# Audio tower on one core: the rolled steady-state loop written out as straight-line iterations

## The reference

```
out = einsum('blfd,fd,fdk->blk', windows(x, 8 taps), filt, W);  h = relu(out + b_k)      # 248 rows x 64
h = h + attention(layernorm(h))      # one head of width 64; softmax over 248 keys; Wo
g = layernorm(h);  logits = g @ Wg + bg + bias;  top 2 of 8 experts, softmax of the two
h = h + sum over experts of combine[e] * (relu(g @ W1[e] + b1[e]) @ W2[e] + b2[e])       # hidden 128
```

## Time and profile before

| | |
|---|---|
| median of 3 runs | 343.15 us (342.94 to 343.67) |
| span of the profiled execution, first to last instruction | 340.8 us |
| PE busy | 307.6 us, 90% of the span, 1486 matmul records |
| DVE busy | 248.6 us, 73% |
| ACT busy | 240.9 us, 71% |
| POOL busy | 92.8 us, 27% |
| granted TensorE clock, mean | 0.959 of full speed |

### The profile page before, as it was taken

How to read it: one execution, slowest core, us unless ns; L and a number is a source line. 1 busy time by engine, 2 the same in 40 slices (tenths; PEclk the granted TensorE clock), 3 DMA queues, 4 the chain that set the end, 5 groups by cost and what they waited for, 6 DMA issues and landing times.

```text
span 340.8 us, 6412 instructions
## 1 busy us (share of the span) xinstructions
PE 307.6 (90%) x1486; PEld 188.0 (55%) x1486; DVE 248.6 (73%) x824; ACT 240.9 (71%) x545; POOL 92.8 (27%) x85
## 2 busy tenths in 40 slices
PE   8587799999999999999999999999999999979754
PEld 8264657565645657475656556474656565534220
DVE  2574747879696979779786969697887979492823
ACT  2427497969686887879686978778786969764520
POOL 1103031513232241515122322315151323132302
PEclk9767899999999999999999999999999999999985
DMA  6120214070614225160706142241707060504050
GB/s 181 50 61 0 63 58 124 17 182 5 159 37 124 73 78 119 29 168 5 191 1 151 45 130 67 81 116 26 171 9 187 2 164 0 147 21 126 12 136 15
DMA packets 17228, 28.38 MB, mean 83 GB/s; under 512 B 3264, under 2 KB 13760, under 8 KB 17216
## 3 DMA queue, kind: packets, MB, share of 16 engines
q1 hardware_dynamic: 16928, 27.98, 32.6%
q10 hardware_dynamic: 288, 0.28, 0.2%
HBM read 21.90 MB, written 2.29 MB: 71 GB/s over the span
## 4 chain that ended last, share of the span: by engine, by line
PE 40%; DVE 22%; issue 16%; ACT 11%; DMA 7%; SPq 1%; DVEq 1%; ACTq 0%; POOL 0%
PE bank_a L787 11%; DMA cb<-weights 5%; DVE ts L252 4%; PE bank_y L846 4%; PE bank_s L897 4%; PE bank_h L836 3%; PE bank_h L837 3%; ACT p L367 3%; ACT hid L376 2%; PE bank_b L904 2%; PE bank_s L804 2%; DVE hsum L637 2%; DVE acc L548 2%; DVE gw L617 2%; PE bank_h L867 2%
## 5 line engine op out<-in xcount | busy, mean ns | idle before, releaser
L376 ACT ACTIVATE hid<-bank_h,col 128x496 f32<-128x496 f32 x128 | 84.0, 674 | 10.5 <-PE bank_h L837 9.2
L846 PE MATMUL bank_y<-hid,w_sb 128*64 128x496 f32 x256 | 68.0, 612 | 3.6 <-DVE acc L548 3.6
L836 PE MATMUL bank_h<-xs,w_hi 128*128 128x496 f32 x128 | 56.2, 439 | 3.0 <-DVE xs L253 2.4
L548 DVE SCALAR_TENSOR_TENSOR acc<-bank_y,col,cb 128x496 f32<-128x496 f32 x64 | 45.4, 730 | 17.3 <-DMA cb<-weights 9.8
L837 PE MATMUL bank_h<-xs,w_lo 128*128 128x496 f32 x128 | 49.8, 389 | 0.0
L262 POOL TENSOR_TENSOR total<-acc 128x496 f32<-128x496 f32 x16 | 20.1, 1256 | 106.7 <-DVE acc L548 106.7
L330 POOL TENSOR_TENSOR p<-p,rmask 124x496 f32<-124x496 f32 x32 | 32.4, 1014 | 51.9 <-DVE rmask L564 51.8
L265 POOL TENSOR_TENSOR total<-total,acc 128x496 f32<-128x496 f32 x16 | 20.0, 1250 | 70.5 <-DVE acc L548 70.5
L836 PEld LDWEIGHTS bank_h<-xs,w_hi 128*128 128x128 f32 x128 | 24.3, 190 | 13.4 <-issue 7.1
L718 DVE SCALAR_TENSOR_TENSOR h<-bank_s,col,h 128x248 f32<-128x248 f32 x16 | 7.6, 476 | 31.9 <-PE bank_s L897 31.9
L367 ACT ACTIVATE p<-bank_s,nmax 124x248 f32<-124x248 f32 x64 | 29.4, 466 | 0.3 <-DVE nmax L555 0.2
(11 more groups left out here) (105 smaller groups left out, 584.8 us busy)
## 6 DMA issues: line engine op xcount, KB each, us to landing
cb<-weights SPq DMA_DIRECT2D x64, 248.0 KB, 4.5
kk<-kk SPq DMA_DIRECT2D x16, 248.0 KB, 2.9
x<-xt SPq DMA_DIRECT2D x15, 256.0 KB, 2.9
out<-h SPq DMA_DIRECT2D x16, 124.0 KB, 1.8
w_sb<-w SPq DMA_DIRECT2D x3, 256.0 KB, 3.6
wtok_sb<-wtok SPq DMA_DIRECT2D x1, 256.0 KB, 2.7
x<-xt ACTq DMA_DIRECT2D x1, 256.0 KB, 3.9
weights<-ct_sb SPq DMA_DIRECT2D x16, 15.5 KB, 1.4
```

The costliest lines, as they stand in the source:

```text
L376: act.activation(hid[2 * (p % 2) + s][:, :], bank_h[s][:, 0:TOK], ACT.Relu, bias=col[:, C_B1 + e:C_B1 + e + 1]).then_inc(hid_ready[s], 1)
L548: dve.scalar_tensor_tensor(out=acc[p % 2][:, :], in0=bank_y[p % 2][:, 0:TOK], scalar=col[:, C_B2 + p:C_B2 + p + 1], in1=cb[:, p, :], op0=A ...
L836: pe.matmul(bank_h[e % 2][:, 0:TOK], w1_hi[:, e, :], xs[par][:, :], start=True, stop=False)
L846: last = pe.matmul(bank_y[p % 2][s * D:s * D + D, 0:TOK], w2_sb[:, 2 * p + s, :], hid[2 * (p % 2) + s][:, :], start=True, stop=True)
```

## The change

The hardware loop goes. `run` calls `iteration` twenty times with Python integers. The flags of each iteration, the order of the work on every engine, the tiles and the awaited values are the same as before. No register is computed, no branch is taken, every wait compares with a constant, and the DRAM addresses of `x` and `out` are constants.

```
-        def run(iteration, eng):
-            iteration(-2, 0, True, False, False, False, False)
-            iteration(-1, 1, True, True, False, False, False)
-            iteration(0, 0, True, True, True, False, False)
-            iteration(1, 1, True, True, True, True, False)
-            with eng.Fori(0, (GROUPS - 4) // 2) as i:
-                iteration(i * 2 + 2, 0, True, True, True, True, True)
-                iteration(i * 2 + 3, 1, True, True, True, True, True)
-            iteration(GROUPS - 2, 0, False, True, True, True, True)
-            iteration(GROUPS - 1, 1, False, False, True, True, True)
-            iteration(GROUPS, 0, False, False, False, True, True)
-            iteration(GROUPS + 1, 1, False, False, False, False, True)
+        def run(iteration):
+            for t in range(-2, GROUPS + 2):
+                iteration(t, t % 2, t + 2 < GROUPS, -1 <= t < GROUPS - 1, 0 <= t < GROUPS, 1 <= t <= GROUPS, t >= 2)
...
-            run(iteration, sp)
+            run(iteration)
```

More of the change, by code:

```diff
@@ L347, in iteration @@
                     add(pool, m, 1)
-            run(iteration, pool)
+            run(iteration)
         @block.scalar
@@ L478, in iteration @@
                     exps(c, 0)
-            run(iteration, act)
+            run(iteration)
         @block.vector
@@ L761, in iteration @@
                     both_weights(n)
-            run(iteration, dve)
+            run(iteration)
         @block.tensor
@@ L989, in iteration @@
                     hidden(n, odd, 0)
-            run(iteration, pe)
+            run(iteration)
 def constants():
```

## The result

The changed kernel takes 334.93 us (median of 4 runs, 334.6 to 335.2). The kernel before, run beside it, took 343.41 us. The ratio is 0.9734, with a 95% interval of 0.9702 to 0.9766. All ratios here are those on record, which compare the fast executions of both kernels, and can differ by some 0.2% from the quotient of two medians.

What follows compares the result with a forecast made beforehand. A ring of waits through DVE, PE and ACT, closing once an iteration, was taken as the bound. From 343.15 us, 3.65 (branches), 1.2 and 0.6 (registers) came off and 1.7 (fetches) was added: 339.4 us, range 336.7 to 342.4.

Steps and rivals of the forecast that it cites:

- Taken branches: Loop turns, where DVE's branch lies bare on the ring of engines: five crossings at 0.73 us, 3.65 us less.
- The even beat: Sign: PE's weight load L904 recurs every 18.2 us or so, no longer at 18.35 and 19.08 us.
- Register instructions: Ahead of waits in twelve iterations: 0.10 us each at PE's L836, 0.05 at ACT's L376; 1.2 and 0.6 us less.
- DVE's other register instructions stand under a running instruction: Step that costed DVE's remaining register instructions at nothing, as running work covers them.
- More code to fetch: Straight code brings some 9 more queue-8 packets that delay awaited DMA transfers: net 1.7 us more, bounds -1.7 to 5.4.
- the 0.50 us left over: Part of the 206.00 us from iteration 2 to 13 beyond the regular intervals, read as a stretched gate-weight store's price.
- the price of a hit: Cost of a code packet falling on a transfer the ring waits for: 0.5 to 1.7 us, taken as 0.6.
- the chance of a hit: Share of an iteration in which a code packet meets an awaited transfer: 6.4 of 18.2 us, 0.35.
- the late hit in iteration 14: Packet at 294 us beside `cb`, DVE idle 1.74 us; might move away, chance about a third, 0.5 us subtracted.
- the fetches are hidden: Rival: all code fetches fall into slack, 337.7 us; chance 0.18.
- Only the branches matter: Rival: semaphore instructions replace the register ones at the same price, 341.2 us; chance 0.22.
- slower: Rival: each queue-8 packet holds the gate weights' round trip through DRAM, 348.5 us at 1.2 us each; chance 0.10.

Runs made afterwards that it cites:

- The moved code: The changed kernel with 40 already met waits added on PE in its first iteration, so later code packets shift: 335.10 us against 344.55 for the kernel before, ratio 0.9724.

## Why the prediction was right, and where it failed

The forecast missed by 339.4 - 334.9 = 4.5 us, and I had given only 0.02 to a time under 336.7. By its own terms:

*Taken branches, 3.65 us: right.* The even beat is there, L538 starts 0.13 us after L619, and the wait for `cb` is gone. DVE straightened alone removes the pause, PE or ACT alone do not, as the argument had it. With the loop gone the intervals across a turn are as short as the others, which is the 5 x 0.73 us; 0.2 of each 0.73 goes with SP straight alone.

*Register instructions, 12 x 0.15 = 1.8 us: the size was 2.93, and the place was wrong.* I put 0.10 on PE's L836 and 0.05 on ACT's L376, and DVE's and SP's at nothing. Both local readings came true: DVE's low part of `xs` is now followed by PE after 0.11 us (before 0.24), and PE's first layer by ACT after 0.04 (before 0.12). But PE straight alone has the quick start at L836 and keeps the 18.37 us beat, and with DVE and SP alone in straight code, PE and ACT as before, the beat is already 18.12 us. So of the 0.27 us, 0.23 are DVE's and SP's (DVE's 0.21 by the quietest interval of DVE alone, 18.14), and 0.04 come with the other three engines. The step that failed is "DVE's other register instructions stand under a running instruction". The kernel's own rows spoke against it: from PE's weight load to the end of DVE's gating there are 13.19 us before (181.76 to 194.95) and 12.97 after (178.09 to 191.06), in which DVE doesn't wait for `cb`. (The idle time of 0.59 and 0.86 us that I read as PE's is that of its weight loads; its matmuls stood 0.19 and 0.45 us there.) I looked for registers at the one link in which a gap stood open, and not at the sum over DVE's stretch. Of the 0.22 us of that stretch 0.09 lie ahead of the first weighing (3.88 us behind the weight load before, 3.79 after); the rest wasn't split further.

*More code to fetch, +1.7 us: the failed step that weighs most.* It came out as -2.0 us, if all that changed there is put down to it: nothing in the loop's time, the 0.50 us left over gone, and 1.49 us less behind it. This is 3.7 of the 4.5 us. The number of packets was right, and the price of a hit was, if anything, too low (DVE waited 1.2 to 2.1 us at each hit in the kernels with PE, or all but SP, straight). What failed is the chance of a hit. I took it from the kernel before, with a `cb` issued 0.97 us ahead of the beat in odd iterations and 1.4 in even ones, and multiplied: nine packets, 0.35 of the time exposed. For that I had counted all of the 5.0 us from `cb`'s issue to its use, while a packet that began 3.1 us or more behind the issue made the first half late in no trace. And the same change that brings the packets lets SP issue `cb` at 1.35 us in every iteration, and in that place packets did nothing (in the forecast's own words, the rival's "new ring with 0.2 us more slack on SP"). With SP's loop kept, four of them hit and ate all of the gain in the loop. The stores that I had counted as exposed did no harm either: three in the loop's time took 1.9 to 2.1 us with no effect, and a fourth, 2.5 us in iteration 15, put `cb` 0.2 us later. The moved code shows that SP's straight code is no shield by itself: one packet in the wrong place still cost 0.7 us. That the four fell just behind that place is luck that I hadn't forecast.

*The 1.49 us behind the loop.* I had given the late hit in iteration 14 a chance of a third to move away. It moved: the queues there list no packet of queue 8, and DVE's idle time before the first weighing is 0.79 us, not 1.74. Eight of the ten kernels that keep PE's loop have that packet, with a second `cb` transfer of 5.2 us or more; those with PE straight have 4.1 to 4.5. So this part (0.95 us) is PE's, and it is a matter of where the packets happen to fall. The other 0.5 us weren't traced; the granted clock behind iteration 13 is 0.92 before and 0.93 after.

*The 0.50 us left over, read as the price of a stretched store: half right.* A stretched store does cost 0.84 us (SP straight alone). But where the store is on time in otherwise unchanged code, the long interval stays, so the reading of the kernel before was incomplete.

*What remains*: 0.57 us more ahead of iteration 2, and 0.22 us less between span and median. Over all runs iteration 2 began anywhere from 67.4 to 71.0 us, so I don't count the 0.57 as an effect of the change. Together: 3.69 + 1.13 - 0.57 + 0.22 = 4.47 us, the whole miss.

Of the rivals, "the fetches are hidden" (337.7 us) named the right mechanism and was still too slow, since it stood on the same 1.8 us of registers and took no credit for the late hit. The rule of the Trainium skill that it leaned on ("Runtime: NRT & Kernel Launch", section "Instruction fetch mechanics": crossing a block is mostly hidden) holds for the changed kernel and not for the one that keeps SP's loop, where four packets lengthened their intervals by 1.4 to 2.0 us, to 19.45 to 20.04 us. "Only the branches matter" fell with the 18.08 us beat, "slower" with the even beat. The low end of the range was the rival's time less a microsecond; adding the terms' own favourable bounds (registers 2.3 + 1.1 us, fetches -1.7) would have given 343.15 - 3.65 - 3.4 - 1.7 = 334.4 us and held the result.

## What to carry to other kernels

In a ring of engines closed by a DMA trip, a stall taken out of one engine shows in full only if the next link keeps up: here DVE alone took 2.2 us off the loop's time, SP alone 0.5, both 6.5, so the sequencer of the bound engine and that of the engine that issues its DMAs are to be straightened together. When a change makes new traffic and new slack at once, price a hit by its place against the transfers after the change, and keep all favourable bounds in the range. Register instructions are found by comparing a whole stretch of the bound engine with its work, not by the one gap that stands open.

## What the runs showed of the hardware that I had not expected

- DVE's taken branch is cheap in a short body and dear in a long one: 0.72 us between the two steps with two iterations a turn (some 170 DVE instructions), 3.25 with four, 3.27 with six. ACT shows no such pause with two or four iterations a turn (0.2 us from its branch to its next instruction), but 2.4 us with six, some 410 instructions. PE, POOL and SP show none. Rolling less tightly gained nothing: six a turn the same time, four a turn 0.8% slower.
- An instruction packet of about 1.2 us on one DMA engine cost from nothing to 2 us of the beat. It hurt when it began 2.3 to 3.06 us behind the first issue of `cb`, and made the first half late in no case from 3.10 us on, so an issue 0.35 to 0.7 us earlier was the difference.
- Stored from ACT's queue instead of SP's, an output of 124 KB took 4.0 us to land instead of 1.7, since it then competes with the transfers that it used to precede.
